# Three units under way in the group sort, an FFN in two PSUM banks, and four edge chunks under way in the segment maximum

## The reference

```python
def _L0_conv_ref(x):                      # x is the channel-normalised input
    x3 = x.reshape(B, M, F)               # M = 4096 tokens of an image, F = 256
    corr = jnp.einsum('bmf,bnf->bmn', x3, x3) / F
    s = -jnp.sort(-corr, axis=-1)         # every row of 4096 in falling order
    ranks = jnp.round(jnp.linspace(1.0, M - 1, 256)).astype(jnp.int32)
    return jnp.take(s, ranks, axis=-1)
...
x = x + _L0_conv_ref(_ln_c(x))
t = t + _L0_ffn_ref(_ln_t(t), ...)
```

## Time and profile before

| what | us |
|---|---|
| median of three executions | 32390.15 |
| the profiled execution | 32599.99 |
| its span | 32598.3 |
| PE busy | 26112.8 (80%) |
| DVE busy | 29043.6 (89%) |
| ACT busy | 21326.7 (65%) |
| POOL busy | 15496.0 (48%) |
| L1287 and L1288, the compare-exchanges | 11641.9 and 11633.6 |
| L1328, the network's absolute values | 14119.6 |
| L1106, the "tile" matrix products | 13524.6 |
| L1584, the gathers of segment_max | 900.6 |

### The profile page before, as it was taken

The page is one execution under the profiler, slowest core; times in us unless marked ns, Lnnn a source line. Parts: engine busy times, 40 slices in busy tenths (PEclk is TensorE's granted clock), DMA queues, the critical chain, the costliest instruction groups (busy, mean ns, idle before and its releaser), DMA issues. The chain is left out here.

```text
span 32598.3 us, 522374 instructions
## 1 busy us (share of the span) xinstructions
PE 26112.8 (80%) x175347; PEld 11892.7 (36%) x175348; DVE 29043.6 (89%) x32774; ACT 21326.7 (65%) x31791; POOL 15496.0 (48%) x9076
## 2 busy tenths in 40 slices
PE   3888888888888888888888888888888888873364
PEld 3555533333333333333333333333333333332364
DVE  6888859999999999999999999999999999997744
ACT  2777777777777777777777777777777777760010
POOL 0000028888888888888888888880000000003510
PEclk8999999999999999999999999999999999996555
DMA  2000000000000000000000000000000000000103
GB/s 87 2 2 2 2 18 6 6 7 7 7 7 12 7 7 6 7 7 7 7 13 6 7 7 6 7 7 6 11 6 6 7 6 6 6 5 13 12 11 129
DMA packets 651263, 396.25 MB, mean 12 GB/s; under 512 B 424844, under 2 KB 604048, under 8 KB 646160
## 3 DMA queue, kind: packets, MB, share of 16 engines
q1 hardware_dynamic: 337746, 311.41, 3.0%
q0 software_dynamic: 290304, 22.40, 1.1%
q10 hardware_dynamic: 20288, 25.70, 0.2%
HBM read 196.48 MB, written 162.34 MB: 11 GB/s over the span
## 5 line engine op out<-in xcount | busy, mean ns | idle before, releaser
L1328 ACT ACTIVATE z<-psum 128x1024 f32<-128x1024 f32 x14208 | 14119.6, 1026 | 3874.4 <-PE psum L1106 2531.0
L1433 POOL DMA_INDIRECT sorted_d<-word_s,place_s x8192 | 14521.6, 1773 | 2646.6 <-issue 2476.6
L1106 PE MATMUL psum<-z,net 64*64 64x512 f32 x103424 | 13524.6, 616 | 2673.1 <-ACT z L1328 2440.0
L1287 DVE TENSOR_TENSOR arena<-arena 128x1536 f32<-128x1536 f32 (+17 forms) x6016 | 11641.9, 1935 | 1194.4 <-ACT arena L1370 598.6
L1288 DVE TENSOR_TENSOR arena<-arena 128x1536 f32<-128x1536 f32 (+17 forms) x6016 | 11633.6, 1934 | 0.0
L1106 PEld LDWEIGHTS psum<-z,net 64*64 64x64 f32 x103424 | 3114.0, 132 | 11895.5 <-issue 11880.4
L1584 POOL DMA_INDIRECT arena<-table_d,arena x752 | 900.6, 1198 | 8297.3 <-issue 7812.2
L1370 ACT ACTIVATE arena<-arena 128x2048 f32<-128x2048 f32 (+15 forms) x5632 | 3221.9, 573 | 987.6 <-DVE arena L1288 543.4
L931 ACT ACTIVATE arena<-cst,arena 128x128 bf16<-128x128 f32 x8320 | 2633.5, 389 | 607.6 <-PE psum L859 509.7
L1113 PE MATMUL psum<-z,net 64*128 64x512 f32 x8192 | 2052.7, 637 | 557.0 <-ACT z L1328 548.9
L1427 POOL DMA_DIRECT2D word_s<-words_d x64 | 37.7, 589 | 4796.3 <-issue 4663.8
(11 more groups left out here) (217 smaller groups left out, 18509.7 us busy)
## 6 DMA issues: line engine op xcount, KB each, us to landing
sorted_d<-word_s,place_s POOLq DMA_INDIRECT x8192
y_d<-ys SPq DMA_DIRECT2D x256, 256.0 KB
arena<-y_d SPq DMA_DIRECT2D x64, 1024.0 KB, 5.6
arena<-in_x SPq DMA_DIRECT2D x34, 512.0 KB, 5.2
x<-in_x SPq DMA_DIRECT2D x65, 256.0 KB
xnt_d<-arena SPq DMA_DIRECT2D x32, 512.0 KB, 3.1
hk_d<-arena SPq DMA_DIRECT2D x32, 512.0 KB, 4.3
arena<-hk_d SPq DMA_DIRECT2D x4, 4096.0 KB
```

The lines of the kernel that those rows point to most:

```text
L1106: last = nc.tensor.matmul(psum[n * HALF:(n + 1) * HALF, 2 * s + r, :], b.net[rr, at:at + HALF], flat[rr, n * BANK:(n + 1) * BANK], start=T ...
L1287: nc.vector.tensor_tensor(hi_out, hi_in, lo_in, ALU.max)
L1328: last = nc.scalar.activation(flat, bank, ACT.Abs)
L1433: pool.indirect_dma_start(out=b.sorted_d[:, :], out_offset=bass.IndirectOffsetOnAxis(ap=place_s[:, s, j:j + 1], axis=0), in_=word_s[:, s, ...
```

## The change

- **Front.** SLOTS goes from 2 to 3: a third z tile and PSUM banks 4 and 5 for it. The 8 units of a pair are now rounds of 3, 3 and 2 units (SLOTS_OF), 36 + 28 + 28 = 92 ticks instead of 120. The first round stays the merged one and has three units, so LO is 1536 instead of 1024 (three eighths of the keys), and a pair has 248 unit steps instead of 240. Semaphore counts are per slot (PER_SLOT, TO_LAST_CORR).
- **FFN.** Hidden units have one bank (6) and both outputs another (7). The hidden layer of an expert is made in two halves, with the GELU of the first half between: `up` at ticks 0 and 3 of the expert, GELU at 1 and 5, `down` at 7 and 8, the copy out at 10; the experts follow at 15 ticks instead of 20.
- **segment_max.** Four chunks under way instead of two. The mask's factor and the sum with the gathered scores are now 16 ScalarE activations of 128x128 each (scale -1e30, bias the gathered score) instead of VectorE's L1522 and L1542. One semaphore counts the four gathers of a slot. SP no longer waits for both chunks before the first store, and PSUM halves go by s % 2.
- **Constants.** A few bf16 constants move from their own tiles into the arena, and the constants' load is two DMAs, which makes the SBUF room.

```diff
-SLOTS = 2
+SLOTS = 3
...
+UNITS = M // WIRES // UNIT_GROUPS
+ROUNDS = (UNITS + SLOTS - 1) // SLOTS
+SLOTS_OF = [min(SLOTS, UNITS - j * SLOTS) for j in range(ROUNDS)]
 MERGED_ROUNDS = 1
-LO = MERGED_ROUNDS * SLOTS * UNIT_GROUPS * WIRES
-ROUNDS = M // WIRES // UNIT_GROUPS // SLOTS
+LO = sum(SLOTS_OF[:MERGED_ROUNDS]) * UNIT_GROUPS * WIRES
...
-    TURN_TICK, TAB_TICK, EXPERT_TICK, EXPERT_TICKS = 24, 27, 31, 20
-    GELU_AFTER, DOWN_AFTER, OUT_AFTER = 3, 6, 9
+    TURN_TICK, TAB_TICK, EXPERT_TICK, EXPERT_TICKS = 18, 21, 24, 15
+    GELU_AFTER, UP_AGAIN, DOWN_AFTER, OUT_AFTER = (1, 5), 3, 7, 10
...
             def up(i, e, m):
                 if m == 0 and e == 0:
                     pe.wait_ge(tab_copied, i + 1)
-                elif m == 0:
-                    pe.wait_ge(gelu_ready, (i * EXPERTS + e) * HC)
+                elif m % 2 == 0:
+                    pe.wait_ge(gelu_ready, (i * EXPERTS + e) * HC + m)
...
             def front(i, tick):
                 j, t = TICK_OF[tick]
                 how, _, meet = FRONT[j][t]
-                for s in range(SLOTS):
-                    act.wait_ge(fe_ready[s], i * PER_PAIR + (tick + 1))
+                for s in range(SLOTS_OF[j]):
+                    act.wait_ge(fe_ready[s], i * PER_SLOT[s] + (tick + 1))
...
-            with dve.Fori(0, pairs) as i:
-                for s in range(2):
-                    for q in range(EQ):
-                        dve.wait_ge(got_in[s][q], (i + 1) * 16)
...
-                    nc.vector.tensor_tensor(
-                        spread[s], other[s].unsqueeze(1).broadcast_to([P, HEADS, EQ, P]),
-                        got[s][:, :, 0:HEADS].rearrange("p q h -> p h q").unsqueeze(3).broadcast_to(
-                            [P, HEADS, EQ, P]), ALU.add).then_inc(spread_ready, 1)
...
+            with dve.Fori(0, rounds) as i:
+                for s in R:
+                    dve.wait_ge(turned[s], i + 1)
+                    tile = dve.value_load(tiles_i[0:1, bass.ds(i * N + s, 1)], min_val=0, max_val=TILES - 1)
+                    nc.vector.tensor_reduce(best[s], psum[:, 4 * (s % 2):4 * (s % 2) + 4, :], AX.X,
+                                            ALU.max).then_inc(best_ready[s % 2], 1)
...
+                    take_apart(i + 1, s)
...
+            with act.Fori(0, rounds) as i:
+                for s in R:
+                    act.wait_ge(other_ready, i * N + (s + 1))
+                    act.wait_ge(turned[s], i)
+                    act.wait_ge(got_in[s], (i + 1) * (16 * EQ))
+                    act.sem_inc(b.settled[4], 1)
+                    for h in range(HEADS):
+                        for q in range(EQ):
+                            last = nc.scalar.activation(spread[s][:, h, q, :], other[s][:, q, :], ACT.Identity,
+                                                        bias=got[s][:, q, h:h + 1], scale=MASKED)
+                    last.then_inc(spread_ready[s], 1)
...
+                    pool.wait_ge(spread_ready[s], i)
                     pool.wait_ge(store_out[s], i * 16)
```

More of the change, by code:

```diff
@@ L233 @@
 PER_PAIR = len(TICK_OF)
-LAST_FIRST = PER_PAIR - len(FRONT[-1]) + 1
+PER_SLOT = [sum(s < SLOTS_OF[j] for j, _ in TICK_OF) for s in range(SLOTS)]
+TO_LAST_CORR = [max(n for n, (j, t) in enumerate(TICK_OF) if t == 0 and s < SLOTS_OF[j]) + 1 for s in range(SLOTS)]
 C_TOTAL = C_NET + NET_COLS
@@ L419, in carve @@
         return v
+    at = LOW_AT + (ECOLS + SUPER) // 2
+    rank_bf, ones_bf = carve(at, [P], BF16), carve(at + 64, [P], BF16)
+    iota_bf = carve(at + 128, [2, P], BF16)
+    counts = carve(at + 256, [64])
+    order_bf = carve(at + 320, [C_ALL - C_WINDOW], BF16)
+    order = carve(at + 512, [C_ALL - C_WINDOW])
+    assert at + 512 + C_ALL - C_WINDOW <= 10 * M
     b = Buffers()
@@ L1137, in table @@
                 pe.wait_ge(tt_ready, i + 1)
+                if not (isinstance(i, int) and i == 0):
+                    pe.wait_ge(y_copied, i * EXPERTS)
                 for g in range(2):
                     for c in range(DC):
-                        last = nc.tensor.matmul(psum[:, 5, g * TAB:(g + 1) * TAB], tt[:, c, g * P:(g + 1) * P],
+                        last = nc.tensor.matmul(psum[:, 7, g * TAB:(g + 1) * TAB], tt[:, c, g * P:(g + 1) * P],
                                                 b.wtab[:, c, :], start=(c == 0), stop=(c == DC - 1))
@@ L1184, in period @@
                 for tick in range(PER_PAIR):
-                    for half in range(SLOTS):
+                    for s in range(SLOTS_OF[TICK_OF[tick][0]]):
                         if has_next:
-                            front(i + 1, tick, half)
-                        if has_last:
-                            ffn_piece(i - 1, tick, half)
+                            front(i + 1, tick, s)
+                        if has_last and s < 2:
+                            ffn_piece(i - 1, tick, s)
             for tick in range(PER_PAIR):
-                for s in range(SLOTS):
+                for s in range(SLOTS_OF[TICK_OF[tick][0]]):
                     front(0, tick, s)
@@ L1411, in _ @@
             for e in range(EXPERTS):
-                hidden(PAIRS - 1, e)
+                for first in (0, 2):
+                    hidden(PAIRS - 1, e, first)
                 expert_out(PAIRS - 1, e)
@@ L1452, in segment_max @@
     sem, carve, psum = b.sem, b.carve, b.psum
+    N = SUM_SLOTS
+    R = range(N)
+    MOST = (MAX_CHUNKS + N) // N
     table = carve(0, [TILES, TAB])
@@ new lines, in _ @@
+            nc.vector.tensor_tensor(top, counted, table[:, :, 0:HEADS], ALU.max).then_inc(counted_ready, 1)
+            dve.wait_ge(counted_ready, 1)
+            with dve.Fori(0, rounds) as i:
+                for s in R:
+                    dve.wait_ge(turned[s], i + 1)
+                    tile = dve.value_load(tiles_i[0:1, bass.ds(i * N + s, 1)], min_val=0, max_val=TILES - 1)
+                    nc.vector.tensor_reduce(best[s], psum[:, 4 * (s % 2):4 * (s % 2) + 4, :], AX.X,
+                                            ALU.max).then_inc(best_ready[s % 2], 1)
+                    dve.wait_ge(spread_ready[s], i + 1)
+                    dve.wait_ge(got_in[s], (i + 1) * (16 * EQ))
+                    take_apart(i + 1, s)
+                    dve.wait_ge(best_ready[s % 2], i * (N // 2) + (s // 2 + 1))
+                    dve.wait_ge(topped, (i * N + s) if s > 0 else i * N)
+                    tops = top[:, bass.ds(tile, 1), :].rearrange("p o h -> p (o h)")
+                    nc.vector.tensor_tensor(tops, tops, best[s], ALU.max).then_inc(topped, 1)
@@ L1559, in _ @@
             pe.wait_ge(setup_in, 64)
-            pairs = pe.value_load(loops_i[0:1, 0:1], min_val=1, max_val=MOST_PAIRS)
-            with pe.Fori(0, pairs) as i:
-                for s in range(2):
-                    pe.wait_ge(spread_ready, i * 2 + (s + 1))
-                    pe.wait_ge(best_ready, i * 4 + (2 * s - 2 if s else 0))
+            rounds = pe.value_load(loops_i[0:1, 1:2], min_val=1, max_val=MOST)
+            with pe.Fori(0, rounds) as i:
+                for s in R:
+                    pe.wait_ge(spread_ready[s], i + 1)
+                    pe.wait_ge(best_ready[s % 2], i * (N // 2) + s // 2 if s >= 2 else i * (N // 2))
                     for h in range(HEADS):
                         for q in range(EQ):
-                            last = nc.tensor.transpose(psum[:, 4 * s + h, q * P:(q + 1) * P], spread[s][:, h, q, :],
-                                                       b.ident)
-                    last.then_inc(turned, 1)
+                            last = nc.tensor.transpose(psum[:, 4 * (s % 2) + h, q * P:(q + 1) * P],
+                                                       spread[s][:, h, q, :], b.ident)
+                    last.then_inc(turned[s], 1)
         @block.gpsimd
@@ L1574, in _ @@
             pool.wait_ge(setup_in, 64)
-            pairs = pool.value_load(loops_i[0:1, 0:1], min_val=1, max_val=MOST_PAIRS)
-            with pool.Fori(0, pairs) as i:
-                for s in range(2):
-                    pool.wait_ge(source_ready, i * 2 + (s + 1))
-                    pool.wait_ge(spread_ready, (i * 2 + s) if s == 0 else i * 2)
+            rounds = pool.value_load(loops_i[0:1, 1:2], min_val=1, max_val=MOST)
+            with pool.Fori(0, rounds) as i:
+                for s in R:
+                    pool.wait_ge(source_ready, i * N + (s + 1))
+                    pool.wait_ge(spread_ready[s], i)
                     pool.wait_ge(store_out[s], i * 16)
```

158 lines of the change are left out of this document (73 added, 85 removed).

## The result

The changed kernel takes 31868.65 us (median of 4, 31848.88 to 31879.93), beside 32390.23 us (32388.24 to 32410.7) for the kernel before: the ratio is 0.9837 with a 95% interval of 0.982 to 0.9854. That is 522 us less, where 1110 were forecast. The profiled execution took 31879.93 us, 31878.2 of it span.

The account below looks back on a forecast made before the run. VectorE was taken to bound pool_rows, and no engine was full in segment_max. Savings of 574 us (pairs and first front), less 6 (FFN), plus 549 (segment_max), scaled to 1110, gave 31280 us, range 30680 to 31900.

Parts of the forecast that it names:

- VectorE's work, -7.5 a pair: pool_rows: the longer merge shortens VectorE's sort stages 0 to 7, saving 7.5 us a pair, to 363.4 us busy.
- TensorE's work, 342: pool_rows: with 248 unit steps instead of 240, a pair needs some 342 us of TensorE, below VectorE's 363.4.
- Gap before stage 49: End of a pair: VectorE's 3.56 us wait for ScalarE's last carries, standing behind the last two ticks, would be gone.
- segment_max, 5.5 a chunk: segment_max: GpSimd's gathers set the pace at 5.5 us a chunk instead of 8.53, 549 us less in all.
- Rival C: segment_max: a chunk costs 7.0 us as gathers, ScalarE and stores are nearly equal in fixed order; 31560 us, chance 0.13.
- First front, -20: The first front, running alone: cheaper tile ticks with three units, less three full units more, make it 20 us shorter.
- I take half, 4.2: Before stage 21: carries outlasting a tick's spare sum to 8.3 us; half, 4.2, is taken as TensorE's delay.
- From there on the ticks get lighter, and the idle time (about 4 us) stays.: pool_rows from stage 21 on: lighter ticks leave VectorE's idle time at about 4 us, keeping the 8.8 us saved a pair.
- The two banks, "nothing": FFN in pool_rows: waiting for the first half's GELU costs nothing, except 6 us in the last pair, which runs alone.
- Rival D: pool_rows: the FFN in two banks stops TensorE at 8 half-GELUs a pair, 29 us; 33070 us, chance 0.05.
- The base: The sum took 389.16 us a pair from the profiled 32599.99 us execution, then scaled its 1117 us by 0.9936 to 1110.
- Rival A: pool_rows: TensorE holds the early stages and a pair stays at 389 us; other gains leave 31820 us, chance 0.17.

Follow-up runs that it names:

- e4: Changed kernel, still four chunks under way, with the mask's factor and 2048-wide sum back on VectorE: 32216.9 us.
- e1: The kernel before, not edited, profiled a second time: 32384.73 us, pairs of 385.7 us in the median.
- e3: Changed kernel with front ticks dealt to the sort stages by cost instead of number: four runs of 30688.1 to 31687.24 us, a pair 367 us.
- e14: The kernel before with only the new FFN (two PSUM banks, hidden blocks in halves), run again on another chip: 32738.08 us.
- e7: e3 plus nine stages a pair where VectorE waits for its own last instruction: 30576.65 us, ratio 0.9444 to the kernel before.
- e9: The kernel before with only the new segment_max: 32269.65 us, beside a kernel before that took 32606.66 there.
- e11: e7 with two rounds (3072 of 4096 keys) merged on TensorE: 38990.22 us, beside a kernel before that took 32606.66 there.

## Why the prediction was half right

- **VectorE's work, -7.5 a pair.** Right: 363.85. **TensorE's work, 342.** Right: 340.98.
- **Gap before stage 49.** Right: 3.9 to 0.3 us.
- **segment_max, 5.5 a chunk.** Right: 5.43. Rival C's 7.0 comes near what e4 measured with the sum on VectorE (7.05), but by luck: C had another reason.
- **First front, -20.** Mis-sized: the sort starts 37 us earlier than in the profile of before, 29.5 earlier than in e1. The tile ticks took TensorE 248.4 us before (234.3 in the prediction) and 212.4 after (208.3): they gave 36 where 26 were counted.
- **"I take half, 4.2", the failed step.** The prediction summed TensorE's ticks 0 to 37 to 152.2 us and added 4.2 us for its pauses, half of the 8.3 by which carries outlast the spare of a tick. Stage 21 was then to start 153.0 us into the pair (15354.1 - 15201.1). The first instructions of stages 0 and 21 in the pair above:

```profile
15096.09 1.49 DVE L1296 TENSOR_TENSOR arena<-arena 128x1280 f32<-128x1280 f32 x1 [1.88 <-issue]
...
15255.68 2.15 DVE L1296 TENSOR_TENSOR arena<-arena 128x1920 f32<-128x1920 f32 x1
```

That is 159.6 us, and 154.6 in e1 (15225.57 - 15070.94). Windows of the same pair say where the 6.6 us are: from the first "corr" to the end of tick 37, and the last 40 us of it.

```profile
15091.80:15252.35 160.55, 150.19 (x996) 65.72 (x996) 141.70 (x116) 130.97 (x162) 135.24 (x67) 1.00 0.03 6
15212.00:15252.35 40.35, 40.34 (x224) 24.61 (x224) 28.86 (x17) 26.46 (x27) 36.39 (x14) 1.00 0.03 7
```

TensorE's list is 150.2 us (152.2 forecast, -2.0), but it pauses for 10.4 us instead of 4.2 (+6.2). It begins 4.3 us ahead of stage 0 instead of 5.0 (+0.7). Stage 21 starts 3.3 us behind tick 37 instead of 1.6 (+1.7): it was not the carry behind tick 37 that held it (done at 15254.97), but the end of stage 20 (15255.68), which had waited for the carry behind tick 36. So the path was nearly right and the durations held; the term for the pauses was too small by more than half. Its ground was that TensorE "can run on with a unit in hand", and where ScalarE is full it can't. Of the 8.3 us by which the pair is longer than the forecast 380.4, these 6.6 lie before stage 21. All the pauses but one of 0.15 us end with ScalarE's activations, and nearly half of them (4.7 us) stand from stage 8 to the start of stage 11, where ScalarE is full (row above). From there on nothing is left to give: in the last 40 us TensorE is busy throughout, and VectorE waits at stages 19 and 20. e3 shows that the place is what costs: the same instructions, dealt out otherwise, and 20 us of idle time are gone.
- **"From there on the ticks get lighter, and the idle time (about 4 us) stays."** Nearly right in size: at stages 34 and 35 VectorE waits 4.8 us in the mean of pairs 3 to 63, where in e1 it waits 3.7 us in all the stages behind 21. The reason given holds only in part: the number of units in a stage does fall, but the next "wires" and "corr" ticks still stand beside stages 34 and 35.
- **The two banks, "nothing".** Wrong in the old order of ticks, where they cost 6 us a pair (e14). Rival D had 29 us, by TensorE waiting for GELUs, and that mechanism isn't in the traces: in the pair of e14, as in that of the changed kernel, no wait of TensorE ends with a GELU. VectorE waits 14.7 us there for carries (7.9 in e1); how the two banks lengthen these waits stays open. What they cost inside the changed kernel was not measured by itself; in e7, with the same banks and the ticks paced, VectorE's whole idle time is 3.5 us.
- **The base.** The pair of 389.16 included 3 us of that execution's own. The sum was scaled by 0.9936 and so near 386.7, so this did little.

Rival A (a pair stays as it is, 31820 us) came nearest to 31869, and its reason was nearest too: 5.75 unit steps a stage where there had been 5, though at first it is ScalarE and not TensorE that is full. The range to 31900 holds 31869 only because it was drawn to take in A.

## What to carry to other kernels

When two engines are tied in one list by number of items, compute each engine's side per stretch, that of the engine between them too, and add the longest of each; a sum over one engine's list tells only the floor. Before taking work off the bounding engine, deal out the other's work by its time: here that gave 21 us a pair with no instruction changed, and the third unit with its longer merge only paid behind it. And when VectorE gets full, look at what GpSimd is doing beside it: leave it a pause.

## What the runs showed of the hardware

Beside VectorE's sort, GpSimd's indirect DMAs get through almost only at the ends of VectorE's two-input instructions. In e7, with VectorE's stages of 2032 and 2040 elements, one scatter follows each:

```profile
14802.46 2.27 DVE L1326 TENSOR_TENSOR arena<-arena 128x2032 f32<-128x2032 f32 x1
14803.74 1.87 POOL L1472 DMA_INDIRECT sorted_d<-word_s,place_s  x1 [0.30 <-issue]
14804.64 2.28 DVE L1325 TENSOR_TENSOR arena<-arena 128x2040 f32<-128x2040 f32 x1
14805.91 1.86 POOL L1472 DMA_INDIRECT sorted_d<-word_s,place_s  x1 [0.30 <-issue]
```

The scatters end at 14805.61 and 14807.77, the VectorE instructions at 14804.73 and 14806.92: 0.88 and 0.85 us apart. Of the 7435 scatters of e7 that start between 6000 and 22000 us, 93% end 0.83 to 0.86 us behind the end of a two-input instruction; from the 10th to the 90th percentile the distance is 0.841 to 0.849 us. Mostly one gets in at each end. Now and then one misses and goes on missing until VectorE pauses, in e3 over some 100 VectorE instructions in a row (the 202.72 us above) and at most 147 (292 us). The mean of the 8192 scatters is 1793 ns in e1, 1898 in the changed kernel, 2568 in e3 and 1807 in e7.

The Trainium skill, SBUF — State Buffer, "Who interferes with whom", infers that `tensor_tensor` does not stall descriptor generation; these runs disagree for indirect DMAs, with a scatter of 1.83 us in the median of e7 and 0.97 at the shortest. The same section also says that a VectorE instruction with two SBUF inputs contends with a GpSimd instruction that reads SBUF; an indirect DMA reads its indices there, and with that the runs agree. They don't tell apart which of the two, the reading or the generation, is held up.

Left open: what slowed the comparison of e9 to e11. While the scatters ran, pairs of e9 took 386 to 395 us (the first 376) and those of e11 393 to 1363, after them 385 to 388 and 385 to 389. In 1000 us of e9's `segment_max` (29700 to 30700) ScalarE paused 181 times, 92.7 us in all and up to 4.3 us at once, where the profile shows nothing that it waited for. No run tells its cause. The best version, e7, is 5.5% faster than the kernel before in two comparisons, but was not run in that one.
